# Attention and int8 FFN on one core: row maxima combined inside the next iteration's turns, on three engines

## The reference

```python
def attn(x, Wq, Wk, Wv, Wo, bo):
    q, k, v = (split_heads(x @ W) for W in (Wq, Wk, Wv))
    scores = einsum('bhqd,bhkd->bhqk', q, k) * HEAD ** -0.5
    scores = where(causal, scores, -inf)
    weights = softmax(scores, axis=-1)
    return merge_heads(einsum('bhqk,bhkd->bhqd', weights, v)) @ Wo + bo

def ffn(lhs, rhs):
    lhs_scale, rhs_scale = absmax_scale(lhs, 2), absmax_scale(rhs, 0)
    q_lhs, q_rhs = int8(round(lhs / lhs_scale)), int8(round(rhs / rhs_scale))
    return (q_lhs @ q_rhs) * lhs_scale * rhs_scale

x = x + attn(layernorm(x), Wq, Wk, Wv, Wo, bo)
x = x + ffn(layernorm(x), rhs)
```

## Time and profile before

| | before |
|---|---|
| median of 3 runs | 1688.91 us |
| the three runs | 1688.57 to 1694.19 us |
| span of the profiled execution | 1686.8 us |
| its own time | the page has the span alone |
| PE, PEld busy | 1603.7 us, 643.5 us |
| DVE, ACT, POOL busy | 1516.0, 1330.8, 290.6 us |
| reductions of turns (L353) | 960 and 128, mean 1216 and 1219 ns |
| exponentials (L1214) | 2304, mean 574 ns |
| value matmuls (L1044) | 8704, mean 391 ns |

### The profile page before, as it was taken

The page is one execution under the profiler, slowest core; times in us unless marked ns, Lnnn a source line. Parts: engine busy times, 40 slices in busy tenths (PEclk is TensorE's granted clock), DMA queues, the critical chain, the costliest instruction groups (busy, mean ns, idle before and its releaser), DMA issues.

```text
span 1686.8 us, 39739 instructions
## 1 busy us (share of the span) xinstructions
PE 1603.7 (95%) x16319; PEld 643.5 (38%) x16319; DVE 1516.0 (90%) x1812; ACT 1330.8 (79%) x2610; POOL 290.6 (17%) x363
## 2 busy tenths in 40 slices
PE   6999999999999999999999999999999999999965
PEld 3445443333333333333333333333333333344433
DVE  4677779999999999999999999999999999678876
ACT  2233338999999999999999999999999999877651
POOL 5333310201020202111111111111112020100120
PEclk9999999999999999999999999999999999999986
DMA  3443320111121212121212112121212143034532
GB/s 108 146 136 117 112 89 12 39 34 40 33 77 37 74 38 68 43 62 43 62 47 59 54 52 59 46 60 46 59 46 67 47 115 88 14 105 136 159 116 70
DMA packets 105609, 118.73 MB, mean 70 GB/s; under 512 B 20688, under 2 KB 87508, under 8 KB 105428
## 3 DMA queue, kind: packets, MB, share of 16 engines
q1 hardware_dynamic: 105428, 116.19, 23.8%
...
## 4 chain that ended last, share of the span: by engine, by line
DVE 54%; PE 27%; issue 1%; ACT 1%; DMA 1%; SPq 1%; POOL 0%; ACTq 0%; DVEq 0%
DVE pmax L353 46%; PE psum L1044 11%; PE psum L1025 6%; DVE pblk L353 4%; PE psum L1084 3%; PE psum L261 3%; PE psum L280 2%; PE psum L275 2%; DMA f_rs<-inverse_sums 1%; DVE V L1323 1%; ACT prob L1214 1%; PE psum L1108 1%; DVE V L1342 1%; DVE V L1330 1%; DVE f_amax L1348 1%
## 5 line engine op out<-in xcount | busy, mean ns | idle before, releaser
L1214 ACT ACTIVATE prob<-psum 128x512 f32<-128x512 f32 (+1 forms) x2304 | 1181.0, 574 | 136.7 <-PE psum L1025 113.2
L353 DVE TENSOR_REDUCE pmax<-psum 128x2 f32<-128x1024 f32 (+1 forms) x960 | 1101.0, 1216 | 13.5 <-PE psum L280 6.5
L1044 PE MATMUL psum<-prob,V 128*32 128x256 f32 x8704 | 676.0, 391 | 0.0
L1025 PE MATMUL psum<-Q,K 50*128 50x512 f16 (+3 forms) x2560 | 464.7, 349 | 3.8 <-ACT prob L1214 1.0
L1277 POOL TENSOR_SCALAR_AFFINE_SELECT prob<-prob 128x512 f32<-128x512 f32 x256 | 160.6, 640 | 1185.3 <-ACT prob L1214 1182.8
L261 PE MATMUL psum<-K,Q 48*128 48x512 f16 x1536 | 298.4, 385 | 13.5 <-DVE pmax L353 13.5
L1044 PEld LDWEIGHTS psum<-prob,V 128*32 128x32 f32 x8704 | 181.5, 108 | 294.2 <-issue 214.1
L1025 PEld LDWEIGHTS psum<-Q,K 50*128 50x128 f16 x2560 | 174.6, 94 | 251.3 <-ACT prob L1214 185.1
L261 PEld LDWEIGHTS psum<-K,Q 48*128 48x128 f16 x1536 | 74.3, 93 | 272.0 <-DVE pmax L353 212.8
L353 DVE TENSOR_REDUCE pblk<-psum 128x8 f32<-128x1024 f32 x128 | 151.8, 1219 | 5.8 <-PE psum L280 5.6
L280 PE MATMUL psum<-K,Q 48*128 48x512 f16 (+3 forms) x1024 | 128.6, 298 | 0.0
...
## 6 DMA issues: line engine op xcount, KB each, us to landing
...
Q<-q_parts SPq DMA_DIRECT2D x128, 64.0 KB, 2.5
K<-k_parts SPq DMA_DIRECT2D x128, 64.0 KB, 2.1
...
```

Of the source, the lines that this page charges most:

```text
L353: nc.vector.tensor_reduce(to, of, axis=AX.X, op=ALU.max).then_inc(M.mx_free, 1)
L1025: m = nc.tensor.matmul(PS[:, SB + i % RING, at:at + n], K[it % 2][rows, pair, kb * P:(kb + 1) * P], Q[it % 2][rows, pair, (c + 1) * CH - n ...
L1044: m = nc.tensor.matmul(PS[32 * h:32 * h + 32, UB, to:to + n], V[:, it // NG * NT + kb, col:col + 32], prob[(it * NSTEP + k) % PRING][:, h, ...
L1214: nc.scalar.activation(prob[g % PRING][:, h, 0:n], PS[:, SB + i % RING, 0:n], ACT.Exp, scale=by).then_inc(exp_done, 1)
```

## The change

The transpose turn of iterations 1 to 14 moves: it now stands behind the fifth turn (`BETWEEN` = 5) of the iteration that follows, and that of 0 and of 15 stays behind its own turns. `pmax` and `pblk` get a second buffer. DVE keeps two pieces: `blocks_to_maxima`, run behind the first turn of the next iteration, and `negated_maxima`, behind its second. POOL makes the two parts in three operations (`split_maxima_on_pool`), ACT copies the transposed parts to `mT` (`take_maxima_on_act`) behind the exponentials of the same pair. The turn is no longer handed back by DVE: `handed_back` counts without it, and PE waits for `mT_ready` ahead of the turn that uses its banks again. The table `BEFORE` isn't changed. Three small buffers for the bias become views of `F.rs`.

```diff
--- before.py
+++ after.py
@@ -95,15 +95,27 @@
 def order_of_turns():
 
-    turns, tail = [], []
+    turns, tail, last = [], [], []
     for it in range(ITS):
-        turns += [(it, kind) for kind in (KINDS if it else sorted(KINDS, key=lambda kind: max(chunks_of(kind))))]
-        tail.append(len(turns))
-        turns.append((it, None))
-    return turns, tail
-
-
-TURNS, TAIL = order_of_turns()
+        kinds = KINDS if it else sorted(KINDS, key=lambda kind: max(chunks_of(kind)))
+        for i, kind in enumerate(kinds):
+            if it >= 2 and i == BETWEEN:
+                tail.append(len(turns))
+                turns.append((it - 1, None))
+            turns.append((it, kind))
+        last.append(len(turns) - 1)
+        if it in (0, ITS - 1):
+            tail.append(len(turns))
+            turns.append((it, None))
+    return turns, tail, last
+
+
+BETWEEN = 5
+TURNS, TAIL, LAST = order_of_turns()
+
+
+def handed_back(n):
+    return sum(kind is not None or it == 0 for it, kind in TURNS[:n])
 
 BEGUN = TAIL[0] + 1 + 12
 RING = 3
@@ -136,19 +148,36 @@
 
 BLOCKS = [(k, block) for k in range(NSTEP) for block in range(len(VALUES[k]))]
 BEHIND_SCORES = sum(len(VALUES[k]) for k in range(NSTEP - LAG, NSTEP))
-assert sum(row[0] + row[2] for row in BEFORE) == TAIL[1] - TAIL[0] and sum(row[1] for row in BEFORE) == len(BLOCKS)
+assert sum(row[0] + row[2] for row in BEFORE) == TAIL[2] - TAIL[1] and sum(row[1] for row in BEFORE) == len(BLOCKS)
 
 def turns_until(it, pair):
 
     front, back = issued_before(0), issued_before(2)
-    base = TAIL[0] + 1 + AHEAD + it * (TAIL[1] - TAIL[0])
+    base = TAIL[0] + 1 + AHEAD + it * (TAIL[2] - TAIL[1])
     return (min(len(TURNS), base + front[pair] + (back[pair - 1] if pair else 0)),
             min(len(TURNS), base + front[pair] + back[pair]))
 
 def blocks_until(it, pair):
     return it * len(BLOCKS) - BEHIND_SCORES + issued_before(1)[pair]
+
+
+def pairs_of_turns():
+
+    out, turn = {}, BEGUN
+    for it in range(ITS):
+        for pair in range(2 * NSTEP):
+            back = turns_until(it, pair)[1]
+            for n in range(turn, back):
+                out[n] = (it, pair)
+            turn = max(turn, back)
+    return out
+
+
+PAIR_OF = pairs_of_turns()
+TAKEN_AT = {PAIR_OF[TAIL[it]]: it for it in range(1, ITS)}
+PARTS_AT = {PAIR_OF[min(LAST[it] + 2, TAIL[it])]: it for it in range(1, ITS)}
 
 
...
@@ -284,7 +317,9 @@
 
     it, kind = TURNS[n]
     if n >= 2:
-        pe.wait_ge(mx_free, n - 1)
+        pe.wait_ge(mx_free, handed_back(n - 1))
+        if TURNS[n - 2][1] is None and TURNS[n - 2][0] >= 1:
+            pe.wait_ge(M.mT_ready, TURNS[n - 2][0] + 1)
     at = MB + 2 * (n % 2)
     if kind is None:
         pe.wait_ge(M.mp_ready, it + 1)
@@ -299,44 +334,70 @@
     m.then_inc(mx_ready, 1)
 
-def combine_maxima(nc, dve, it, M):
-
-    pmax, pblk, negm, mparts, comb, COMB = M.pmax, M.pblk, M.negm, M.mparts, M.comb, M.COMB
-    dve.wait_ge(M.mx_free, TAIL[it])
-    blk = pblk[:].rearrange("p f h a j -> p (f h a) j")
-    top = pmax[:].rearrange("p f h (a t) j -> p (f h a) t j", t=TPC)
+def blocks_to_maxima(nc, dve, it, M):
+
+    dve.wait_ge(M.mx_free, handed_back(LAST[it] + 1))
+    blk = M.pblk[it % 2][:].rearrange("p f h a j -> p (f h a) j")
+    top = M.pmax[it % 2][:].rearrange("p f h (a t) j -> p (f h a) t j", t=TPC)
     nc.vector.tensor_reduce(top[:, :, 2, 3], blk[:, :, 0:3], axis=AX.X, op=ALU.max)
-    nc.vector.tensor_copy(top[:, :, 0, 3], blk[:, :, 3]).then_inc(comb, 1)
-    dve.wait_ge(comb, it * COMB + 1)
-    nc.vector.tensor_reduce(negm[:], pmax[:].rearrange("p f h q j -> p (f h q) j"), axis=AX.X, op=ALU.max,
-                            negate=True).then_inc(comb, 1)
-    dve.wait_ge(comb, it * COMB + 2)
-    nc.vector.tensor_scalar(mparts[:, 0, :], negm[:], 1.0 / ONE, None, ALU.mult).then_inc(comb, 1)
-    dve.wait_ge(comb, it * COMB + 3)
+    nc.vector.tensor_copy(top[:, :, 0, 3], blk[:, :, 3]).then_inc(M.blocks_in, 1)
+
+
+def negated_maxima(nc, dve, it, M):
+
+    dve.wait_ge(M.blocks_in, it + 1)
+    if it >= 1:
+        dve.wait_ge(M.mp_ready, it)
+    nc.vector.tensor_reduce(M.negm[:], M.pmax[it % 2][:].rearrange("p f h q j -> p (f h q) j"), axis=AX.X, op=ALU.max,
+                            negate=True).then_inc(M.negm_ready, 1)
+
+
+def split_maxima(nc, dve, M):
+
+    negm, mparts = M.negm, M.mparts
+    dve.wait_ge(M.negm_ready, 1)
+    nc.vector.tensor_scalar(mparts[:, 0, :], negm[:], 1.0 / ONE, None, ALU.mult).then_inc(M.first_part, 1)
+    dve.wait_ge(M.first_part, 1)
     nc.vector.scalar_tensor_tensor(out=mparts[:, 1, :], in0=negm[:], scalar=1.0 / ONE, in1=mparts[:, 0, :],
                                    op0=ALU.mult, op1=ALU.subtract).then_inc(M.mp_ready, 1)
 
+def split_maxima_on_pool(nc, pool, it, M):
+
+    negm, mparts, scaled = M.negm, M.mparts, M.scaled
+    pool.wait_ge(M.negm_ready, it + 1)
+    pool.wait_ge(M.mT_ready, it)
+    nc.gpsimd.tensor_scalar(scaled[:], negm[:], 1.0 / ONE, 1.0, ALU.mult, ALU.mult).then_inc(M.first_part, 1)
+    pool.wait_ge(M.first_part, 3 * it - 1)
+    nc.gpsimd.tensor_copy(mparts[:, 0, :], scaled[:]).then_inc(M.first_part, 1)
+    pool.wait_ge(M.first_part, 3 * it)
+    nc.gpsimd.tensor_tensor(mparts[:, 1, :], scaled[:], mparts[:, 0, :], ALU.subtract).then_inc(M.first_part, 1)
+    pool.wait_ge(M.first_part, 3 * it + 1)
+    pool.sem_inc(M.mp_ready, 1)
+
+
 def take_maxima(nc, dve, it, PS, M):
 
     n = TAIL[it]
-    if it >= 1:
-        dve.wait_ge(M.mrows_in, it * M.MROWS)
     dve.wait_ge(M.mx_ready, n + 1)
     nc.vector.tensor_copy(M.mT[:], PS[:, M.MB + 2 * (n % 2), :].bitcast(F16)[:, 0:P]).then_inc(M.mx_free, 1)
     dve.wait_ge(M.mx_free, n + 1)
     dve.sem_inc(M.mT_ready, 1)
 
+def take_maxima_on_act(nc, act, it, PS, M):
+
+    n = TAIL[it]
+    act.wait_ge(M.mrows_in, it * M.MROWS)
+    act.wait_ge(M.mx_ready, n + 1)
+    nc.scalar.copy(M.mT[:], PS[:, M.MB + 2 * (n % 2), :].bitcast(F16)[:, 0:P]).then_inc(M.mT_ready, 1)
+
+
 def max_turn_on_dve(nc, dve, n, PS, M):
 
-    pmax, pblk = M.pmax, M.pblk
     it, kind = TURNS[n]
+    pmax, pblk = M.pmax[it % 2], M.pblk[it % 2]
     at = M.MB + 2 * (n % 2)
-    if kind is None:
-        combine_maxima(nc, dve, it, M)
-        take_maxima(nc, dve, it, PS, M)
-        return
     of = PS[:, at:at + 2, :]
     if kind[0] == "off":
         _, pair, qt, kc = kind
@@ -691,13 +754,14 @@
 
             statistics(0)
             variance(0)
-            nc.vector.memset(M.pmax[:], NEG).then_inc(pmax_set, 1)
+            for s in range(2):
+                nc.vector.memset(M.pmax[s][:], NEG).then_inc(pmax_set, 1)
             one_over_std(0)
             normalise(0)
             scale_weights()
             statistics(1)
             variance(1)
-            dve.wait_ge(pmax_set, 1)
+            dve.wait_ge(pmax_set, 2)
             one_over_std(1)
             normalise(1)
             for n in range(NC):
...
@@ -1121,7 +1186,8 @@
             turn, block = BEGUN, 0
             for it in range(ITS):
                 if it + 1 == ITS:
-                    pe.wait_ge(mx_free, len(TURNS))
+                    pe.wait_ge(mx_free, handed_back(len(TURNS)))
+                    pe.wait_ge(M.mT_ready, ITS)
                     for c in range(NCH):
                         pe.wait_ge(chunk_in[it % 2][c], (it // 2 + 1) * (16 * LOADS))
                 for k in range(NSTEP):
@@ -1213,6 +1279,8 @@
                             act.wait_ge(p_free, g - PRING + 1)
                         nc.scalar.activation(prob[g % PRING][:, h, 0:n], PS[:, SB + i % RING, 0:n],
                                              ACT.Exp, scale=by).then_inc(exp_done, 1)
+                        if h % 2 == 1 and (it, 2 * k + h // 2) in TAKEN_AT:
+                            take_maxima_on_act(nc, act, TAKEN_AT[it, 2 * k + h // 2], PS, M)
                         if h % 2 == 1 and it + 1 == ITS:
                             for p, u in units_at(2 * k + h // 2):
                                 unit(p, u)
@@ -1269,6 +1337,9 @@
                             unit(n // 3, n % 3)
                     if k == ENDS[1] + 1 and 2 <= it < WHOLE + 2:
                         normalise_group(it - 2)
+                    for pair in (2 * k, 2 * k + 1):
+                        if (it, pair) in PARTS_AT:
+                            split_maxima_on_pool(nc, pool, PARTS_AT[it, pair], M)
                     if parts[0][0] < TPC * c:
                         continue
                     pool.wait_ge(exp_done, it * NS + G * k + G)
@@ -1387,9 +1458,16 @@
 
             for n in range(BEGUN, len(TURNS)):
                 it = TURNS[n][0]
-                if it >= 2 and n == (TAIL[it] + TAIL[it - 1]) // 2:
+                if it >= 2 and n == (LAST[it] + LAST[it - 1]) // 2:
                     invert(it - 2)
-                max_turn_on_dve(nc, dve, n, PS, M)
+                if TURNS[n][1] is not None:
+                    max_turn_on_dve(nc, dve, n, PS, M)
```

(15 more changed lines are left out.)

22 lines of the change are left out of this document (13 added, 9 removed).

## The result

The changed kernel takes **1704.3 us** (median of 4 runs, 1702.1 to 1710.5); the kernel before 1689.9 (4 runs, the three shown ahead and one more). The ratio is 1.0085, with a 95% interval of 1.0067 to 1.0102: slower, by 0.9%. The profiled execution of the changed kernel took 1702.07 us, its span is 1700.4 us, 13.6 more than before.

A forecast was written before the change was run, and what follows sets the result against it. DVE leads over most of the chain, but around an iteration's end PE has no turns to give. 9.1 (iterations) + 0.3 (row DMAs) + 0.4 (last iteration) = 9.8 us on 1688.9 gave 1698.7 us, range 1686 to 1707.

The forecast's parts named there:

- Steps 1 to 3: End of an iteration: DVE idles 2.2 us ahead of the first diagonal turn, PE stands 0.95 us ahead of the third.
- Step 4: DVE's diagonal reductions, then the transpose turn, which waits for the fourth diagonal turn's bank pair and starts at 732.03.
- X released by a reduction: Sign of being right: in the chain, the transpose turn waits for a DVE reduction to free its bank pair.
- Step 5: The first turn behind the transpose turn waits for the fifth diagonal turn's bank pair; DVE stands 0.5 us again.
- step 3: Behind the third diagonal turn ACT has caught up, so scores take 0.32; they start 1.19 late, the values 0.95.
- Step 6: Later turns, until DVE has its backlog again: PE's start there moves from 737.76 to 738.41, the iteration 0.65 us longer.
- the term of 0.65: Lengthening of each iteration in us, over 14 iterations 9.1 us; bounds 0.5 to 0.87 each.
- Row DMAs: SP's four row DMAs start later, behind ACT's copy; some iterations' first scores wait up to 0.5, 0.3 us in all.
- rival C: Slower still: the maxima rows land late in each iteration, adding 7 us, 1705.7 us; chance 0.11.
- Iteration 15: Last iteration: transpose turn comes 0.3 late behind POOL's splits, and ACT copies between exponentials: 0.4 us, bounds 0 and 1.5.
- Rival A: Faster: DVE decides throughout, each iteration shortens by its relief, 14 x 1.76 = 24.6, 1664.3 us; milder form 1681.9; chance 0.12.
- Rival B: The same: the walk holds, but small waits of PE and ACT absorb more loss: 14 x 0.3, 1693 us; chance 0.27.

The follow-up runs named there:

- the better order: Kernel before with 13 rows of the slot table changed: 1687.1 us; changed kernel with these rows and the first diagonal turn one slot earlier: 1692.5 us.

## Why the prediction was right, and where it was off

The direction, the mechanism and the place hold; the time (1698.7) is 5.6 us short of the median and the range (1686 to 1707) holds it.

- **What bounds it.** Right. DVE idle ahead of d0: 2.2 forecast, 2.18 measured.
- **Steps 1 to 3.** d0's reduction 726.76 (726.77 measured), d1 on PE 726.77 (726.77), d2 728.03 (728.05), the scores 728.42 (728.45), the values 728.74 (728.77). The wait ahead of d2 was named as a release of a bank pair by a reduction, and that is what the row shows.
- **Step 4.** X 732.03 (732.04), d4's reduction 731.9 (731.82). "X needs the pair of d3, free at 731.97" is not what held it, though: d3's reduction ended 0.13 us ahead of X, the trace shows no wait of X, and the scores ahead of it had themselves stood 0.20 for ACT. So the sign "X released by a reduction" failed, and the time is right by luck: the pair was free 0.06 earlier than walked, and PE came 0.17 later.
- **Step 5 is where the size went off.** o5 on PE 733.16 (733.26), its reduction 733.58 (733.69). The walk left out that the second score matmul behind X waits for ACT: the scores take 0.49 to the values instead of 0.32. In step 3 I had let ACT catch up with PE; here it hadn't. The walk also gave the pair of d4, free at 733.1, as what o5 waits for. It is free at 733.04 and PE comes at 733.26, straight from the values ahead: what holds o5 is that X and its scores stand ahead of it on PE. The hole ahead of o5 is 0.66, not 0.5.
- **Step 6.** o7 735.6 and 736.0 (735.69 and 736.12), o8 737.15 (737.27), o10 738.41 (738.54). So the term of 0.65 measured 0.78 at o10, inside the bounds of 0.5 to 0.87. "Nothing gives the 0.65 back" holds, and 0.05 more is added behind o10 by the reciprocal, which the change moves one reduction earlier and of which the prediction says nothing: 0.83, 14 x 0.18 = 2.5 us more than taken.
- **POOL.** 1.1 us taken, 0.98 measured with the gaps; ready at 730.7, as forecast; nothing.
- **ACT's copy.** 0.3 taken, 0.27 measured; it ends at 733.87 (734.0 forecast); nothing.
- **Row DMAs.** 0.3 us in all taken; one iteration waited, for 0.28, and its period is 0.37 longer. The case of late rows each time (rival C) didn't occur, but its price was far too low: X two turns later brings it about, and it costs 14 x 2.5 us on average, not 7: 1.2 for the wait alone, where I had taken 0.5, and the clock.
- **Iteration 15.** 0.4 taken, 0.36 measured.
- **Rival A** is refuted by the result, and most plainly in the old place with the early copy (81.49): there every step of the difference is named, and DVE's relief isn't among them. With d0 earlier (81.18) and with the better order (81.02 against 80.92) it buys nothing either, though there the hole at o5 is part of the sum. Its price of 14 x 1.76 was too high in any case as work taken off DVE: 0.65 of the 1.76 are instructions. The Trainium skill (Perfetto Trace Analysis, Identifying the Most-Contended Engine) would have pointed at VectorE, 89% busy against a LDWEIGHTS share of 38% on PE. The traces don't bear that out here: at the place that was changed that engine waits for PE.
- **Rival B**, that small waits take up more of the loss, had the wrong sign: the small wait in step 5 was added to it.
- **The rest.** 9.8 us forecast, 13.6 in the spans: 2.5 from the term above, 0.2 ahead of the first period, which go with the granted clock, and 1.1 in the last phase, which I can't put down to the change.

Open: what the hole at o5 costs by itself, what the reciprocal costs in a run that moves it alone, and the 1.1 us of the last phase.
